# A ternary feed-forward kernel: down weights and residual tiles loaded in pieces behind each pair's weight blocks

## The reference

```python
h = gelu(embedding @ W0 + b0); h = gelu(h @ W1 + b1)
att = softmax(h @ W2 + b2)                                  # 64 x 8
out = einsum('boi,bih->boh', einsum('bk,koi->boi', att, weight), x) + (att @ bias_k)[:, :, None]
def bitlinear(x, w):                                        # ternary weights
    scale = mean(abs(w)); q = round(clip(w / (scale + EPS), -1, 1))
    return x @ (q * scale).T
inter = bitlinear(out, w_gate) * bitlinear(out, w_up)       # 4096 x 2752
return x + bitlinear(inter, w_down)                         # 4096 x 1024
```

## Time and profile before

| | |
|---|---|
| median of 3 runs | 1700.57 us (1699.85 to 1701.57) |
| the profiled execution | 1700.44 us, of which the span from its first to its last instruction is 1698.6 us |
| PE busy | 1679.6 us, 99% of the span |
| DVE, ACT, POOL busy | 1222.2, 700.2 and 128.2 us |
| granted TensorE clock | 0.998 |
| DMA moved | 236.08 MB, mean 139 GB/s |
| one chunk from 2 on | about 200.4 us (group 1 of chunk 1 starts at 463.4, that of chunk 2 at 663.8) |

### The profile page before, as it was taken

The page is one execution under the profiler, slowest core; times in us unless marked ns, Lnnn a source line. Parts: engine busy times, 40 slices in busy tenths (PEclk is TensorE's granted clock), DMA queues, the critical chain, the costliest instruction groups (busy, mean ns, idle before and its releaser), DMA issues.

```text
span 1698.6 us, 36174 instructions
## 1 busy us (share of the span) xinstructions
PE 1679.6 (99%) x14360; PEld 1217.0 (72%) x14368; DVE 1222.2 (72%) x2038; ACT 700.2 (41%) x1451; POOL 128.2 (8%) x198
## 2 busy tenths in 40 slices
PE   7999999999999999999999999999999999999999
PEld 5554554876859687795958969597776968678694
DVE  6888896686777767776686757867677766876474
ACT  6877742231425234351443514353343524434140
POOL 0010003682300000000000000000000000000000
PEclk9999999999999999999999999999999999999999
DMA  8667724541436223461234504264143522336031
GB/s 348 253 221 254 250 93 165 195 149 32 157 109 203 87 63 128 142 204 47 78 137 153 199 28 150 82 206 135 44 148 134 174 85 74 117 106 204 29 128 50
DMA packets 112024, 236.08 MB, mean 139 GB/s; under 512 B 13312, under 2 KB 53184, under 8 KB 111712
## 3 DMA queue, kind: packets, MB, share of 16 engines
q1 hardware_dynamic: 107104, 214.21, 37.1%
q0 software_dynamic: 4144, 19.34, 3.0%
q10 hardware_dynamic: 592, 0.09, 0.0%
HBM read 197.60 MB, written 36.00 MB: 138 GB/s over the span
## 4 chain that ended last, share of the span: by engine, by line
PE 95%; DMA 2%; SPq 1%; DVE 1%; issue 0%; ACT 0%; DVEq 0%
PE ps L1017 35%; PE ps L1170 25%; PE ps L786 17%; PE ps L1029 15%; PE ps L1129 2%; SPq L595 1%; DMA wuT<-in_L_ffn_w_gate_dram 1%; PE ps L893 1%; DMA wgT<-wcomb 1%; DVE msk L1777 0%; DVE xa L1848 0%; DVE prod L1815 0%; ACT wdT L1368 0%; SPq L563 0%; DVE xa L1851 0%
## 5 line engine op out<-in xcount | busy, mean ns | idle before, releaser
L1017 PE MATMUL ps<-yp,wgT 128*128 128x256 f16 x2820 | 634.0, 273 | 0.6 <-DMA wgT<-wcomb 0.6
L1017 PE MATMUL ps<-wuT,wgT 128*128 128x256 f16 x2820 | 634.0, 273 | 0.0
L1170 PE MATMUL ps<-wdT,inter 128*128 128x512 fp8e4 x1960 | 434.4, 379 | 0.4
L1170 PEld LDWEIGHTS ps<-wdT,inter 128*128 128x128 f16 x1960 | 191.2, 98 | 227.4 <-DVE inter L2105 0.6
L1017 PEld LDWEIGHTS ps<-yp,wgT 128*128 128x128 fp8e4 x2820 | 276.0, 98 | 31.4 <-DMA wgT<-wcomb 0.8
L1017 PEld LDWEIGHTS ps<-wuT,wgT 128*128 128x128 fp8e4 x2820 | 275.9, 98 | 31.2
L2128 DVE SCALAR_TENSOR_TENSOR xr<-ps,osc,xr 128x512 f32<-128x512 f32 x210 | 157.0, 749 | 124.1 <-PE ps L1170 100.7
L1506 ACT COPY raw<-ps 128x512 f32<-128x512 f32 (+1 forms) x77 | 44.1, 573 | 289.3 <-PE ps L1017 287.7
L1029 PE MATMUL ps<-yp,wgT 128*128 128x128 f16 x744 | 123.0, 219 | 1.4 <-issue 1.4
L1029 PE MATMUL ps<-wuT,wgT 128*128 128x128 f16 x744 | 123.0, 219 | 0.0
L2040 DVE TENSOR_TENSOR wdT<-ps,msk 128x512 f32<-128x512 f32 (+1 forms) x77 | 51.4, 667 | 77.9 <-PE ps L1017 77.9
(11 more groups left out here) (286 smaller groups left out, 2517.1 us busy)
## 6 DMA issues: line engine op xcount, KB each, us to landing
wgT<-wcomb SPq DMA_DIRECT2D x70, 640.0 KB, 5.0
wdT<-dcomb SPq DMA_DIRECT2D x14, 2240.0 KB, 9.5
wgT<-wcomb SPq DMA_DIRECT2D x70, 256.0 KB, 2.7
xa<-in_x_dram SPq DMA_DIRECT2D x8, 2048.0 KB, 9.2
xr<-in_x_dram SPq DMA_DIRECT2D x32, 512.0 KB, 4.2
out_dram<-xr SPq DMA_DIRECT2D x64, 256.0 KB, 2.0
wcomb<-xa POOLq DMA_DIRECT2D x17, 448.0 KB, 3.0
g_r<-wsub SPq DMA_DIRECT2D x54, 128.0 KB, 2.8
```

Source lines behind the costliest of these rows:

```text
L1017: last = nc.tensor.matmul(out, w, operand(i, OPERAND[what])[:, k, :], start=(start and h + k + i == 0), stop=(k == KQ - 1 and i == 1), ski ...
L1170: last = nc.tensor.matmul(bank[:, :], x, wd_block(p, BLOCK[what]), start=(what in ("P1", "P2", "P5") and q + i == 0), stop=(q == GRP - 1 a ...
```

## The change

`down_load` no longer loads a half at once, but one part of 448 KB (`down_load(g, q)`), and `load_res` loads one tile of 512 KB for each call in place of two. In chunks 2 to 7 part q of group 0 goes behind the late load of pair q + 2, so that the parts stand at p = 2 to 6. In all chunks the four residual tiles go behind the late loads of p = 3 to 6, and the parts of group 1 behind those of p = 7 to 10, the fifth directly behind the fourth. Chunk 1 still gets group 0's weights ahead of its pairs, now as five loads. TensorE's wait counts five landings for each half.

```diff
-            def load_res(c, i):
-                for t in (2 * i, 2 * i + 1):
-                    sp.wait_ge(s_st[t], 16 * HB * c)
-                    sp.dma_start(xr[:, t, :], xt[c * NT + t]).then_inc(s_res[t], 16)
+            def load_res(c, t):
+                sp.wait_ge(s_st[t], 16 * HB * c)
+                sp.dma_start(xr[:, t, :], xt[c * NT + t]).then_inc(s_res[t], 16)
...
-            def down_load(g):
-                dst = wd_flat[:, 0:GRP * PART].bitcast(f32).rearrange("p (q n) -> p q n", q=GRP)
-                sp.dma_start(dst, dcomb[g * GRP:(g + 1) * GRP].rearrange("q p n -> p q n")).then_inc(s_wd, 16)
+            def down_load(g, q):
+                sp.dma_start(wd_flat[:, q * PART:(q + 1) * PART].bitcast(f32), dcomb[g * GRP + q]).then_inc(s_wd, 16)
...
                     sp.wait_ge(s_m3, n + p - 1)
                     late_load(p)
-                    if p == 3 and not (isinstance(c, int) and c == FIRST):
-                        sp.wait_ge(s_dn, DN * FIRST + ND2 * (c - FIRST))
-                        down_load(0)
-                    if p in (4, 5):
-                        load_res(c, p - 4)
-                    if p == NPR:
-                        sp.wait_ge(s_dn, DN * FIRST + ND2 * (c - FIRST) + len(DOWN[0]))
-                        down_load(1)
+                    if p in range(2, 7) and not (isinstance(c, int) and c == FIRST):
+                        if p == 2:
+                            sp.wait_ge(s_dn, DN * FIRST + ND2 * (c - FIRST))
+                        down_load(0, p - 2)
+                    if p in range(3, 7):
+                        load_res(c, p - 3)
+                    if p in range(7, NS):
+                        if p == 7:
+                            sp.wait_ge(s_dn, DN * FIRST + ND2 * (c - FIRST) + len(DOWN[0]))
+                        down_load(1, p - 7)
+                down_load(1, GRP - 1)
...
-            down_load(0)
+            for q in range(GRP):
+                down_load(0, q)
...
-                        pe.wait_ge(s_wd, 16 * (2 * (c - FIRST) + g + 1))
+                        pe.wait_ge(s_wd, 16 * GRP * (2 * (c - FIRST) + g + 1))
```

## The result

The changed kernel takes 1712.83 us (median of 5 runs, 1709.12 to 1714.66) against 1700.05 us (5 runs, 1699.67 to 1701.57) for the kernel before. The ratio is 1.0066, 95% interval 1.0054 to 1.0077: slower by about 11 us. Forecast were +6.3 us and at most 1709.5 us, so the sign was right and the size too small. The runs also spread over 5.5 us where those of before spread over 2 (in the later sessions the kernel before itself spread over 2.7 us in 17 runs and over 4.7 us in 16).

The account below looks back on a forecast made before the run. TensorE was taken to bound the kernel, with only 2 us of removable waits. Six new waits (7.5 us) less a 1.2 us gain made +6.3 us, from 1700.57 to 1706.9 us, range 1702.0 to 1709.5.

Parts of the forecast that it names:

- The place and the mechanism: First matmul of group 0, chunks 2 to 7: TensorE waits for the fifth part, 7.5 us in total.
- The gain at pair 4: Chunk 7: without the big load in front, pair 4's early load lands in time, saving a 1.2 us wait once.
- The other moves at nothing: Parts 0 to 3, group 1's parts and the residual tiles at their new places were to cost 0.
- the 0.5 us allowed: Start of chunk 1, five issues replacing one: put at 0, with 0.5 us either way.
- I take 3.65 us: Time from issue to landing of group 0's fifth part behind pair 6's late load.
- I use 1.25: Time in us that TensorE stands still at group 0 in each of chunks 2 to 7.
- six times: 6 x 1.25 = 7.5 us: The same wait at group 0 in each of chunks 2 to 7, bounds 3.2 and 10.0 us.
- the upper bound of 1.67: Longest wait in us forecast for one group 0, from a residual tile's 4.1 us.
- the upper bound of 10.0: Most in us that the six waits at group 0 together were forecast to cost.
- At full clock in every slice: Reading of the earlier profile: TensorE busy 1679.6 us of a 1698.6 us span, at full clock throughout.
- The lower bound: Shortest wait forecast at one group 0, 0.53 us, from POOL's 448 KB stores at 2.9 us.
- The rival of a short wait: Fifth part lands as if nothing stood in front: +2.0 us, 1702.6 us; chance 0.14.

Follow-up runs that it names:

- e2_only_fifth_late: Kernel before with loads where they stood but split into parts, only group 0's fifth part moved to p = 6 behind the late load; 1711.34 us, ratio 1.0066.
- e1_fifth_at_p5: Changed kernel with group 0's fifth part moved to p = 5, behind the fourth; 1699.68 us, ratio 0.9993.
- e5_fifth_before_m3: Changed kernel with the fifth part at p = 6 issued ahead of SP's wait for P3 of pair 4; 1701.33 us, ratio 1.0002.
- a0_again: The changed kernel measured once more, unaltered; 1711.41 us, ratio 1.0071.
- e4_longer_wait: Changed kernel with residual tile 3 issued ahead of the fifth part at p = 6; 1730.89 us, ratio 1.0177.
- e9_longer_busy: Changed kernel with residual tile 3 ahead of the fifth part and 26 discarded matmuls before TensorE's wait in chunks 2 to 7; 1717.65 us, ratio 1.0104.
- e3_fifth_ahead_of_late: Changed kernel with the fifth part issued ahead of the late load, still behind the wait for P3 of pair 4; 1704.79 us, ratio 1.0030.
- e8_residual_away: Changed kernel with residual tile 3 moved from p = 6 to p = 5, behind tile 2; 1710.13 us, ratio 1.0048.
- e11_shift_fetch_32: Changed kernel with 16 small discarded matmuls (32 instructions) once, ahead of group 0 of chunk 1; 1712.15 us, ratio 1.0060.

## Why the prediction was right and wrong

**The place and the mechanism: right, and shown.** The fifth part of group 0, issued behind the wait for P3 of pair 4, is the cost: e2_only_fifth_late has it alone and is as slow, e1_fifth_at_p5 and e5_fifth_before_m3 lack it and are level with the kernel before. The waits stand where they were forecast, six of them, released by the load that was named.

**The gain at pair 4: right.** The wait of the earlier trace rows is gone in the profile, and comes back when four parts stand at p = 3.

**The other moves at nothing: right** within 0.15% (e1_fifth_at_p5), and in that trace each chunk from 2 on takes what it took before, but for the gain at pair 4. At the start of chunk 1 the wait grew by 0.3 us, inside the 0.5 us allowed.

**The size of a wait: "I take 3.65 us" and "I use 1.25".** For an undisturbed part this was good and even high: 3.5 us, and a shift of 1.04 to 1.09 us in four chunks of six. What failed is the step "six times: 6 x 1.25 = 7.5 us": the six are not alike. In two of six chunks in the profile, three in a0_again, an instruction transfer makes the part 4.0 to 5.2 us long, up to 2.75 us of shift, beyond the upper bound of 1.67. The six together were 8.5 us in the profile and 10.2 us in a0_again, the latter over the upper bound of 10.0 for the sum. The trace of before had this to show. I read the late load of chunk 2, 2.6 us, and took it for all. The late load at the same place in chunk 4, issued at 971.21, was

```profile
wgT<-wcomb SPq DMA_DIRECT2D x1, 256.0 KB, 4.2
```

so the same disturbance stood in it, hidden because nothing waited for that load.

**The clock: missing.** The sum was made of waits alone and put the clock at nothing without a reason. "At full clock in every slice" also read too much into the row, whose 9 is 90% or more: within its first slice the kernel before has 6.8 us at half clock,

```profile
27.90:34.60 6.70, 6.11 (x30) 5.80 (x30) 6.70 (x11) 6.70 (x14) 0.00 (x0) 0.50 1.03 410
```

while from chunk 1 to the end it has none. In the profile of the changed kernel the clock costs 1.7 us. That a wait can bring it down, and what this costs, are shown by e4_longer_wait, where all six waits of 2.5 to 4.2 us went with half clock, and e9_longer_busy, where none did with TensorE kept busy. For the changed kernel's own waits, of 0.9 to 2.6 us, the traces show it once in some executions and not at all in others.

**What stays open.** The profiled execution, at 1709.51 us, is accounted for, and lies at the upper end of the range; the median, 1712.83 us, is 3.3 us above it and outside. The runs that make the median have no trace. Three things vary between the kept traces and could add up to this: the sum of the six shifts (8.5 or 10.2 us with the same kernel), half clock behind a wait (1.7 us or nothing), and the start of the kernel (2.3 us), which has nothing to do with the change. The lower clocks of the longer runs (0.995 to 0.997 against 0.998) do not tell them apart. So the waits' own half clock as the reason for the spread, which is theory 2 for the changed kernel, is not shown.

**The lower bound** of 0.53 us a wait, from POOL's 448 KB stores at 2.9 us, was too low: the same size as a load by SP takes 3.4 us with nothing in front (e3_fifth_ahead_of_late). The rival of a short wait fell with it. The Trainium skill's estimate for a part alone (DMA: Bandwidth & Descriptors, Anatomy of one DMA), 3.05 us, is 0.3 to 0.4 us too low for these loads; the page measured its fit on transfers that GpSimd issues, and POOL's 2.9 us is near it, but these are issued by SP. Had the parts been undisturbed and the clock full, the change would have cost 6 x 1.06 - 1.4 + 0.3 = 5.3 us.

## What to carry to other kernels

Splitting a big load and spreading its pieces is free only up to the last piece: ask for the last piece behind which wait it is issued, and how much of the consumer's own work lies between that wait and the need. Here 2.9 us stood against 3.9 us, and one wait earlier in the same queue costs nothing. Price such a wait with the like transfers in the trace at that place, in every iteration and not in one, and look for what else was in flight with the slow ones. Where TensorE is otherwise never idle, count with half of a stretch at the lower clock behind a wait of over 2 us: here it came behind some waits of 2.2 to 2.6 us and behind all six in the kernel with waits of 2.5 to 4.2 us. And before a run's clock is put down to a change, look in a trace at where it was low.

## What was not expected of the hardware

- Waits of 2.2, 2.3 and 2.6 us (e8_residual_away, e2_only_fifth_late, the changed kernel) were each followed by 3.4 us at half clock; waits of 2.4 and 2.1 us (a0_again, e11_shift_fetch_32) were not, and those of about 1 us never were. All six of e4_longer_wait, 2.5 to 4.2 us, went with it, two of them with 6.8 us.
- 26 matmuls whose results are thrown away, in front of each of six waits, made a kernel 13 us faster (1730.89 to 1717.65 us): most of it is clock, some of it that the parts landed earlier.
- A transfer of instructions of 16 KB, under way within some 2 us of the issue of a 448 KB load behind a late load, goes with 3.8 to 5.2 us for the load in place of 3.4 to 3.7 (15 and 27 parts). A few dozen instructions more, once, in chunk 1, move it to another chunk.
